# A block of attention and routed experts on one core: the order of the loads before the first expert, and a combination split in two around a VectorE product

## The chip, the cores and the metric

The kernel runs on one core of a Trainium2 chip. The metric is device time in microseconds (us) of one execution. The kernel before took 1906.12 us, the median of 3 runs (1905.55 to 1906.73).

## The reference

Input is x of 4 batches, 1024 rows each, 512 wide (4096 rows, that is 32 tiles of 128 rows). The first half is an attention-like block without softmax over rows (products with 512x512 weights, a shift by one row). What matters here is the second half, a layer of 8 experts with the best 2 chosen for each row, and one shared expert:

```python
h = _layernorm(x) * (1 + cb) + sb
# ffn, with F = 352, FS = 704, E = 8, K = 2
shared_out = (silu(h @ Wsg.T) * (h @ Wsu.T)) @ Wsd.T
scores = softmax(h @ Wr.T)
topk_scores, topk_idx = top_k(scores, 2)
out_e = (silu(h @ Wg[e].T) * (h @ Wu[e].T)) @ Wd[e].T      # for each expert e
routed_out = sum over the two chosen e of topk_scores * out_e
x = x + gb * (routed_out + shared_out)
```

All of it is in float32. The kernel gets it from products of three terms: each operand is split into a high part (rounded by ScalarE) and a low part (the difference, on VectorE), and TensorE adds high*high, high*low and low*high.

## The kernel before

The work of the second half is cut into units. A unit is 128 rows through one set of 352 hidden columns. For each unit TensorE does, in this order: it turns the previous unit's hidden rows (`turn_hid`, 3 transposes, L2027), multiplies this unit's rows with the gate and up weights (`up`, 24 matmuls of 352 columns, L566 to L568), and multiplies the previous unit's turned rows with the down weights (`down`, 9 matmuls, L2032 to L2034). ScalarE does `hidhi` (the high part of the turned rows, L1199) and `silu` (L1205). VectorE does `hidlo` (the low part, L1632) and `hid_of` (the product of silu(gate) and up, called `hid`, L1628). TensorE's next `turn_hid` waits for `hid`, and its `down` waits for `hid_lo`.

The shared expert is two halves of 352 columns, so one tile of rows is two units. Tiles 0 to 13 (FU = 14) are done beside the attention part, tiles 14 to 17 after it (`EARLY`, up to SPLIT = 18), then come the 39 routed tiles of 256 rows (`ROUTED`, two units each, one expert each), and then tiles 18 to 31 of the shared expert (`LATE`). Rows were scattered by expert into a buffer in DRAM (`expert_in_rows`) by GpSimd's indirect DMAs, and results go to `expert_out_rows`.

Before a routed tile can start, its rows must be loaded (`load_rows`, 2 DMAs of 256 KB) and its expert's weights (`load_expert`, 3 DMAs of 1408, 512 and 192 KB, into one of two buffers `raw`), which ScalarE and VectorE then split. All of these are issued by SyncE (SP), in the order of its program. After the last rows are read for the scatter (L837), SP's program before goes: eight pads of zero rows (`pad_rows`, L873 and L874, 512 KB each, one behind each expert's rows), the weights of routed tiles 0 and 1, then fourteen loads of what tiles 0 to 13 have so far (`base`, L897, 256 KB each, each waiting for the one two before it), then a wait for the pads and the scatters, and the rows of routed tile 0. The loop over the routed tiles follows, and behind it fourteen loads of residual rows for tiles 18 to 31 (`load_residual`).

In the LATE part the routed results are combined with the shared ones: 16 pairs of tiles, numbered q. GpSimd gathers the two results of each row (4 indirect DMAs a pair). ScalarE multiplies the first with its score (`first_product`, L1339 and L1342). VectorE adds the second times its score (L1866, two instructions), multiplies by the gate of the batch (L1871) and adds to the base rows (L1881). `combined_at(q)` says at which tile and half this stands, on ScalarE and on VectorE alike; before it is tile 19 + q // 2, half q % 2.

Engines take their instructions in the order written. ScalarE's part of the LATE loop, which the change does not touch, is this:

```python
for half in range(2):
    ...
    hidhi_before(*LATE.before(t, half))
    silu(LATE.unit(t, half), bank_of(LATE, half))
    if half and n + 2 < NT:
        load_turned(LATE, n + 2)
    ...
    for q in range(NT // 2):
        if combined_at(q) == (n, half):
            first_product(q)
```

Of the kernel before, what the change touches and what calls it, by code (L numbers as in the profile page):

```python
# [20 lines left out]
P = 128  # L21
# [4 lines left out]
NT = N // P  # L26
# [8 lines left out]
NJ = (2 * N + E * (R - 1)) // R  # L35
NU = NJ * R // P
FU = 14
SPLIT = 18
# [82 lines left out]
ROUTED = Part(0, NJ, 2 * SPLIT, EARLY)  # L121
# [16 lines left out]

def combined_at(q):

    return SPLIT + 1 + q // 2, q % 2


COMBINED_FIRST = next(q for q in range(NT // 2) if 2 * q + 1 >= combined_at(q)[0])
# [15 lines left out]
def sweep(eng, count, lead, lag, body, first=0):  # L160

    low = first + lag + 2 + lag % 2
    high = count - lead - (count - lead) % 2
    for t in range(first - lead, low):
        body(Tile(None, t, count, first))
    with eng.Fori(0, (high - low) // 2) as k:
        for j in range(2):
            body(Tile(k, low + j, count, first))
    for t in range(high, count + lag):
        body(Tile(None, t, count, first))  # L170
# [6 lines left out]
def one_by_one(part, lead, lag, body):  # L177
    for n in range(part.first - lead, part.count + lag):
        body(Tile(None, n, part.count, part.first))
# [45 lines left out]
def build(nc, io, out):  # L225
# [3 lines left out]
    def scratch(name, shape, dt=F32):  # L229
        return nc.dram_tensor(name, shape, dt).ap()  # L230
# [4 lines left out]
    xres_d = scratch("xres_rows", [N, D])  # L235
# [6 lines left out]
    with ctx:  # L242
        def sem(name):
            return ctx.enter_context(nc.semaphore(name))

        def pair_of_sems(name):
            return [sem(f"{name}{p}") for p in range(2)]
# [46 lines left out]
        first = w1_shelf  # L294
# [121 lines left out]
        base = fourth.put("base", [P, NT, D])  # L416
# [40 lines left out]
        rs_out = sem("rs_out")  # L457
        fb_in = pair_of_sems("fb_in")
# [157 lines left out]
        def load_raw(sp, i, gu_rows, dn_rows):  # L616

            whole = FK - 1
            sp.dma_start(raw[i][:, 0:C * GU], gu_rows).then_inc(raw_in[i], 16)
            sp.dma_start(raw[i][:, C * GU:C * GU + whole * D].rearrange("p (k d) -> p k d", k=whole),  # L620
                         dn_rows[0:whole * P, :].rearrange("(k p) d -> p k d", p=P)).then_inc(raw_in[i], 16)
            sp.dma_start(raw[i][0:F - whole * P, C * GU + whole * D:RAW], dn_rows[whole * P:F, :]).then_inc(raw_in[i], 16)
# [8 lines left out]
        FIRST = ROUTED.tile(0)  # L631
# [8 lines left out]
        def bank_of(part, half):  # L640

            return 0 if part is FUSED else half
# [5 lines left out]
        def _(sp):  # L648
# [181 lines left out]
            def load_scattered(n):  # L830
                if n == 0:
                    sp.wait_ge(route_ones, 2)
                    sp.wait_ge(route_const, 4)
                if n >= 2:
                    sp.wait_ge(sc_out[n % 2], 32 * (n // 2))
                sp.wait_ge(h3_out[n % 2], 16 * (n // 2) + 16)
                sp.dma_start(sc_rows[:, n % 2, :], h3_d[n * P:(n + 1) * P, :]).then_inc(sc_in[n % 2], 16)  # L837
# [21 lines left out]
            def load_residual(n):  # L859
                order = n - FU  # L860
                if order >= 2:
                    sp.wait_ge(sr_in[order % 2], 16 * (order // 2))
                sp.dma_start(base[:, n, :], xres_d[n * P:(n + 1) * P, :]).then_inc(sr_in[order % 2], 16)

            def load_expert(t):
                e = sp.value_load(eid[0:1, bass.ds(t.n, 1)], min_val=0, max_val=E - 1)
                if t.back(2).real():
                    sp.wait_ge(*rw_lo_vec.done(t.back(2).n, "dn_lo"))
                load_raw(sp, t.p, io["ex_gu"][bass.ds(e, 1)].rearrange("a p c -> (a p) c"),
                         io["ex_dn"][bass.ds(e, 1)].rearrange("a f d -> (a f) d"))  # L870
# [14 lines left out]
            for n in range(26, NT):  # L885
                load_scattered(n)
            sp.wait_ge(route_done, 1)
            sp.wait_ge(pads_zero, 1)
            for e in range(E):
                pad_rows(e)  # L890
            for first in range(2):
                load_expert(ROUTED.tile(first))
            sp.wait_ge(rs_out, 16 * FU)
            for n in range(FU):
                if n >= 2:
                    sp.wait_ge(fb_in[n % 2], 16 * (n // 2))
                sp.dma_start(base[:, n, :], xres_d[n * P:(n + 1) * P, :]).then_inc(fb_in[n % 2], 16)  # L897


            def load_rows(t):  # L900
                first = sp.value_load(row_of_tile[0:1, bass.ds(t.n, 1)], min_val=0, max_val=XS_ROWS - R)
# [7 lines left out]
            for p in range(2):  # L909
                sp.wait_ge(sc_out[p], 32 * (NT // 2))  # L910

            def load_shared_again(i):

                t = Tile(None, NJ + i, NJ + 2)
                sp.wait_ge(*rw_lo_vec.done(t.n - 2, "dn_lo"))
                load_raw(sp, t.p, io["sh_gu"][i], io["sh_dn"][i])

            def routed_step(t):
                if t.back(-1).real():
                    load_rows(t.back(-1))  # L920
                if t.real() and t.back(-2).real():
                    load_expert(t.back(-2))
                if t.pair is None and t.n in (NJ - 2, NJ - 1):
                    load_shared_again(t.n - (NJ - 2))

            sweep(sp, NJ, 2, 0, routed_step)


            for n in range(SPLIT, NT):
                load_residual(n)  # L930
            for q in range(COMBINED_FIRST):
                sp.wait_ge(*cb_vec.done(q, "out"))
                sp.dma_start(out_d[2 * q * P:2 * (q + 1) * P, :].rearrange("(a p) d -> p a d", p=P),
# [429 lines left out]
        def _(dve):  # L1363
# [262 lines left out]
            def hid_rows(u, half, bank):  # L1626
                dve.wait_ge(*u_act.done(u, "silu"))
                dve.tensor_tensor(hid[:, half, 0:F], PS_U[bank][:, 0:F], sg_t[:], ALU.mult).then_inc(u_vec.sem_of["hid"], 1)  # L1628
# [154 lines left out]
            def hid_of(part, t, half):  # L1783
                dve.wait_ge(*u_pe.done(part.unit(t, half) - 2, "turned"))
                hid_rows(part.unit(t, half), half, bank_of(part, half))

            def hidlo(part, t, half):
                hidlo_rows(part.unit(t, half))
# [69 lines left out]
            sweep_part(dve, ROUTED, 1, 1, routed_step)  # L1858


            def combine(q):
                p = q % 2
                dve.wait_ge(y2_in[p], 32 * (q // 2) + 32)
                dve.wait_ge(*cb_act.done(q, "first"))
                for a in range(2):
                    last = dve.scalar_tensor_tensor(cb_out[:, p, a, :], cb_y2[:, p, a, :], w2[:, 2 * q + a, :],  # L1866
                                                    cb_out[:, p, a, :], ALU.mult, ALU.add)
                last.then_inc(cb_vec.sem, 1)
                dve.wait_ge(*cb_vec.done(q, "both"))
                batch = q // (TPB // 2)  # L1870
                dve.tensor_tensor(cb_out[:, p], cb_out[:, p], mod3[:, batch:batch + 1, :].to_broadcast([P, 2, D]),  # L1871
                                  ALU.mult).then_inc(cb_vec.sem, 1)
                dve.wait_ge(*cb_vec.done(q, "gated"))
                rows = base[:, 2 * q:2 * q + 2, :]
                if q >= COMBINED_FIRST:
                    for n in range(2 * q, 2 * q + 2):
                        order = n - FU
                        dve.wait_ge(sr_in[order % 2], 16 * (order // 2) + 16)
                else:
                    dve.wait_ge(*base_vec.done(2 * q + 1, "base"))  # L1880
                dve.tensor_tensor(rows if q >= COMBINED_FIRST else cb_out[:, p], cb_out[:, p], rows,  # L1881
                                  ALU.add).then_inc(cb_vec.sem, 1)

            for n in range(SPLIT, NT):
                t = LATE.tile(n)
                for half in range(2):
                    before = LATE.before(t, half)
                    hidlo(*before)
                    hid_of(LATE, t, half)
                    if n == SPLIT:  # L1890
                        expert_lo(Tile(None, NJ + 1, NJ + 2), half)
                    if before[0] is ROUTED:
                        y_of_unit(*before[1:])
                    if n == SPLIT + 1 and not half:
                        for k in range(2):
                            dve.wait_ge(fb_in[k], 16 * len(range(k, FU, 2)))
                    pairs = [q for q in range(NT // 2) if combined_at(q) == (n, half)]
                    for q in pairs:
                        if q >= COMBINED_FIRST:
                            combine(q)  # L1900
                    if before[0] is LATE and not half:
                        base_of(LATE, n - 1)
                    for q in pairs:
                        if q < COMBINED_FIRST:
                            combine(q)
            hidlo(LATE, LATE.last(), 1)
            base_of(LATE, NT - 1)

# [331 lines left out]
```

## Time and profile before

| | |
|---|---|
| median of 3 runs | 1906.12 us |
| the profiled execution | 1902.73 us, its span 1901.0 us |
| mean granted TensorE clock | 0.956 of 2.4 GHz |
| busy share of the span | TensorE (PE) 91%, VectorE (DVE) 71%, ScalarE (ACT) 40%, GpSimd (POOL) 29% |
| chain that ended last | PE 65%, DVE 19%, DMA 5%, issue 4%, POOL 3% |

A PE that is busy 91% of the time leaves little: the places to look at are the stretches where it stands still. The profile names for an idle stretch the instruction behind it and what released that. The clock (PEclk) is what the chip granted: 1.00 is 2.4 GHz and 0.50 is 1.2 GHz.

### The profile page before, as it was taken

Reading aid. Unit: us, or ns where it says so; the run is one execution under the profiler, and the core shown is the slowest. Engines: PE = TensorE matmul, PEld = TensorE weight load, DVE = VectorE, ACT = ScalarE, POOL = GpSimd, SP = SyncE. Lnnn points to the kernel's source line nnn. Section 1 sums busy time; section 2 is a strip of 40 time slices with the busy share of each in tenths; the row PEclk is TensorE's granted clock in tenths of the full one; section 3 lists DMA queues with packets and bytes.
Section 4 is the critical chain, followed back from the end, with each engine's and each line's share of the span. In section 5 each row is a group of like instructions: output and inputs, shape, how many; then the busy total and the mean of one; then the engine's idle time right before and its main releaser. Section 6 shows DMA issues by size and latency. Waiting matters only on the chain.

```text
span 1901.0 us, 28565 instructions
## 1 busy us (share of the span) xinstructions
PE 1726.2 (91%) x9093; PEld 1494.5 (79%) x9093; DVE 1347.9 (71%) x2468; ACT 767.5 (40%) x1147; POOL 548.4 (29%) x631
## 2 busy tenths in 40 slices
PE   4599999997678999999999884999999999997898
PEld 0488888885567878878878784999999999986888
DVE  4899999984587788777776533667666666756752
ACT  2333333341334545545454212455554545432221
POOL 0344444441354434545545420000000000006620
PEclk8699999999789999999999996999999999999999
DMA  9422222211533434545545786766667676677731
GB/s 333 144 91 88 88 88 88 88 66 67 180 111 124 143 139 150 200 151 192 206 147 183 272 287 187 251 237 242 240 233 251 230 255 230 247 243 246 244 118 45
DMA packets 141362, 338.74 MB, mean 178 GB/s; under 512 B 20649, under 2 KB 20649, under 8 KB 135777
## 3 DMA queue, kind: packets, MB, share of 16 engines
q1 hardware_dynamic: 110592, 250.15, 38.4%
q10 hardware_dynamic: 20448, 54.01, 7.7%
q0 software_dynamic: 10240, 33.56, 5.1%
q8 instruction: 42, 0.69, 0.1%
q14 instruction: 40, 0.32, 0.1%
HBM read 230.14 MB, written 107.53 MB: 178 GB/s over the span
## 4 chain that ended last, share of the span: by engine, by line
PE 65%; DVE 19%; DMA 5%; issue 4%; POOL 3%; ACT 2%; SPq 1%; another core or an unknown queue 0%; DVEq 0%; ACTq 0%; POOLq 0%
PE bank L566 16%; PE bank L567 15%; PE bank L568 15%; DVE mix L1544 6%; PE bank L577 4%; PE bank L2032 4%; PE bank L2034 4%; PE bank L2033 4%; PE bank L2027 2%; DVE xm_lo L1550 1%; DMA base<-xres_rows 1%; ACT xm_hi L1147 1%; POOL diff L1000 1%; DMA stage<-in_w_k 1%; DVE k_lo L1557 1%
## 5 line engine op out<-in xcount | busy, mean ns | idle before, releaser
L566 PE MATMUL bank<-gu_hi,ex_x_hl 128*128 128x352 f32 x1136 | 380.3, 335 | 2.7 <-DVE gu_lo L1810 1.9
L568 PE MATMUL bank<-gu_hi,ex_x_hl 128*128 128x352 f32 x1136 | 368.0, 324 | 0.0
L567 PE MATMUL bank<-gu_lo,ex_x_hl 128*128 128x352 f32 x1136 | 367.9, 324 | 0.0
L1081 POOL DMA_INDIRECT raw<-expert_out_rows,out_slots x64 | 74.2, 1159 | 624.7 <-DMA expert_out_rows<-y_rows 588.4
L1628 DVE TENSOR_TENSOR hid<-bank,sg_t 128x352 f32<-128x352 f32 x142 | 74.0, 521 | 231.6 <-ACT sg_t L1205 225.3
L566 PEld LDWEIGHTS bank<-gu_hi,ex_x_hl 128*128 128x128 f32 x1136 | 215.7, 190 | 3.4 <-DVE gu_lo L1810 2.1
L1544 DVE SCALAR_TENSOR_TENSOR mix<-diff,vecs,h2T 128x128 f32<-128x128 f32 x256 | 160.7, 696 | 80.0 <-POOL diff L1000 80.0
L567 PEld LDWEIGHTS bank<-gu_lo,ex_x_hl 128*128 128x128 f32 x1136 | 215.8, 190 | 0.0
L568 PEld LDWEIGHTS bank<-gu_hi,ex_x_hl 128*128 128x128 f32 x1136 | 215.1, 189 | 0.0
L2032 PE MATMUL bank<-dn_hi,hid_hi 128*128 128x512 f32 x426 | 172.7, 405 | 23.5 <-DVE hid_lo L1632 17.2
L1205 ACT ACTIVATE sg_t<-bank 128x352 f32<-128x352 f32 x142 | 66.1, 465 | 306.8 <-PE bank L568 290.7
L2034 PE MATMUL bank<-dn_hi,hid_lo 128*128 128x512 f32 x426 | 170.5, 400 | 0.0
L2033 PE MATMUL bank<-dn_lo,hid_hi 128*128 128x512 f32 x426 | 169.3, 397 | 0.0
L1810 DVE TENSOR_TENSOR gu_lo<-raw,gu_hi 128x2816 fp32r<-128x2816 f32 x41 | 126.4, 3082 | 7.1 <-ACT gu_hi L1281 7.1
L1139 ACT ACTIVATE h2T<-bank,vecs 128x128 f32<-128x128 f32 x128 | 48.2, 457 | 186.0 <-PE bank L577 186.0
L566 PE MATMUL bank<-w_r_hi,xm_hi 128*128 128x512 f32 x256 | 109.0, 426 | 9.9 <-DVE h1T L1467 9.9
L1281 ACT ACTIVATE gu_hi<-raw 128x2816 fp32r<-128x2816 f32 x41 | 105.0, 2560 | 19.8 <-issue 12.5
L2032 PEld LDWEIGHTS bank<-dn_hi,hid_hi 128*128 128x128 f32 x426 | 81.4, 191 | 38.6 <-issue 20.9
L567 PE MATMUL bank<-w_r_lo,xm_hi 128*128 128x512 f32 x256 | 105.8, 413 | 0.0
L568 PE MATMUL bank<-w_r_hi,xm_lo 128*128 128x512 f32 x256 | 105.3, 411 | 0.0
L566 PE MATMUL bank<-w_k_hi,xm_hi 128*128 128x512 f32 x256 | 104.1, 407 | 0.0
L1476 DVE SCALAR_TENSOR_TENSOR stage<-diff,vecs,h1T 128x128 f32<-128x128 f32 x384 | 102.9, 346 | 0.0
(229 smaller groups left out, 3942.0 us busy)
## 6 DMA issues: line engine op xcount, KB each, us to landing
raw<-in_ex_gu SPq DMA_DIRECT2D x39, 1408.0 KB, 6.6
raw<-in_ex_dn SPq DMA_DIRECT2D x39, 512.0 KB, 7.4
ex_x<-expert_in_rows SPq DMA_DIRECT2D x78, 256.0 KB, 2.7
expert_out_rows<-y_rows ACTq DMA_DIRECT2D x78, 256.0 KB, 5.4
h_rows<-h_t SPq DMA_DIRECT2D x64, 256.0 KB, 2.4
h_turned<-h_hl ACTq DMA_DIRECT2D x32, 512.0 KB
ex_x_hl<-h_turned ACTq DMA_DIRECT2D x32, 512.0 KB
x_t<-in_x SPq DMA_DIRECT2D x32, 256.0 KB, 2.6
```

Of the source, the lines that this page charges most:

```text
L566: pe.matmul(acc, act_hi[i], w_hi[i], start=(i == 0), stop=False)
L567: pe.matmul(acc, act_hi[i], w_lo[i], start=False, stop=False)
L568: last = pe.matmul(acc, act_lo[i], w_hi[i], start=False, stop=(i == chunks - 1))
L577: last = pe.transpose(bank[:, c * P:(c + 1) * P], rows[:, c * P:(c + 1) * P], ident[:])
L1081: pool.indirect_dma_start(rows[:, pair % 2, a, :], None, ys_d, bass.IndirectOffsetOnAxis(ap=out_slots[:, k, n:n + 1], axis=0)).then_inc(ar ...
L1281: act.activation(flat_of(gu_hi, t), raw[t.p][:, 0:C * GU], ACT.Copy).then_inc(rw_hi_act.sem, 1)
L1476: last = dve.scalar_tensor_tensor(mix1[:, m, c, :], diff1[:, c, :], vecs[:, mu, c:c + 1], h1T[:, t.p, c, 0:P], ALU.mult, ALU.add)
L1544: last = dve.scalar_tensor_tensor(mix2[:, m, c, :], diff2[:, c, :], vecs[:, mu, c:c + 1], h2T[:, t.p, c, 0:P], ALU.mult, ALU.add)
L1810: dve.tensor_tensor(flat_of(w_lo, t), raw[t.p][:, cols], flat_of(w_hi, t).bitcast(F32), ALU.subtract).then_inc(rw_lo_vec.sem, 1)
L2032: pe.matmul(PS_Y[:], hid_hi[:, c, :], dn_hi[w][:, c, :], start=start and c == 0, stop=False)
L2033: pe.matmul(PS_Y[:], hid_hi[:, c, :], dn_lo[w][:, c, :], start=False, stop=False)
L2034: last = pe.matmul(PS_Y[:], hid_lo[:, c, :], dn_hi[w][:, c, :], start=False, stop=stop and c == FK - 1)
```

## The change

It has three parts.

- SyncE's order ahead of the routed part. The first expert's weights are loaded ahead of the eight pads. Behind the pads come the wait for pads and scatters and the first tile's rows, and only then the second tile's weights. The fourteen loads of `base` and the fourteen residual loads are taken apart: routed step n issues one of them, for n from 0 to 13 and from 18 to 31, behind its weights. SP's loop over the routed tiles is written out (`one_by_one` in the place of `sweep`).
- `combined_at(q)` is one tile later, 20 + q // 2. With it COMBINED_FIRST, from which on the result is added into `base` and stored from there, goes from 12 to 13.
- VectorE's `combine(q)` is cut in two. `weighted(q)` (the two scored additions and the gate) stands between `hidlo` and `hid_of`, and `combined(q)` (the addition to the base rows) behind `hid_of`.

```diff
 def combined_at(q):
-    return SPLIT + 1 + q // 2, q % 2
+    return SPLIT + 2 + q // 2, q % 2
...
             sp.wait_ge(route_done, 1)
+            load_expert(FIRST)
             sp.wait_ge(pads_zero, 1)
             for e in range(E):
                 pad_rows(e)
-            for first in range(2):
-                load_expert(ROUTED.tile(first))
-            sp.wait_ge(rs_out, 16 * FU)
-            for n in range(FU):
-                if n >= 2:
-                    sp.wait_ge(fb_in[n % 2], 16 * (n // 2))
-                sp.dma_start(base[:, n, :], xres_d[n * P:(n + 1) * P, :]).then_inc(fb_in[n % 2], 16)
...
             for p in range(2):
                 sp.wait_ge(sc_out[p], 32 * (NT // 2))
+            load_rows(FIRST)
+            load_expert(ROUTED.tile(1))
+            sp.wait_ge(rs_out, 16 * FU)
+            def load_base(n):
+                if n >= 2:
+                    sp.wait_ge(fb_in[n % 2], 16 * (n // 2))
+                sp.dma_start(base[:, n, :], xres_d[n * P:(n + 1) * P, :]).then_inc(fb_in[n % 2], 16)
...
-                if t.pair is None and t.n in (NJ - 2, NJ - 1):
+                if t.n >= NJ - 2:
                     load_shared_again(t.n - (NJ - 2))
-            sweep(sp, NJ, 2, 0, routed_step)
-            for n in range(SPLIT, NT):
-                load_residual(n)
+                if t.n < FU:
+                    load_base(t.n)
+                elif SPLIT <= t.n < NT:
+                    load_residual(t.n)
+            one_by_one(ROUTED, 0, 0, routed_step)
...
-            def combine(q):
+            def weighted(q):
...
+            def combined(q):
+                p = q % 2
                 dve.wait_ge(*cb_vec.done(q, "gated"))
...
                     hidlo(*before)
+                    for q in pairs:
+                        weighted(q)
                     hid_of(LATE, t, half)
...
                     for q in pairs:
                         if q >= COMBINED_FIRST:
-                            combine(q)
+                            combined(q)
                     if before[0] is LATE and not half:
                         base_of(LATE, n - 1)
                     for q in pairs:
                         if q < COMBINED_FIRST:
-                            combine(q)
+                            combined(q)
```

On SyncE, before, this stood behind the last pad (L897 are the base loads, of which the first three of fourteen are shown):

```order
L874 DMA expert_in_rows<-y_rows 128x2x512
L866 TENSOR_LOAD eid
L866 ISA x2
L619 ISA
L619 DMA raw_177<-in_ex_gu 128x2816
L620 ISA
L620 DMA raw_177<-in_ex_dn 128x2x512
...
L897 DMA base<-xres_rows 128x512 [waits rs_out]
L897 DMA base<-xres_rows 128x512
L897 DMA base<-xres_rows 128x512 [waits fb_in0]
...
L901 TENSOR_LOAD row_of_tile [waits sc_out0,sc_out1,pad_out,h3T_out]
```

And in the changed kernel, with line numbers of its own (L894 and L898 load rows, L912 is the base load of a step):

```order
L874 DMA expert_in_rows<-y_rows 128x2x512
L894 TENSOR_LOAD row_of_tile [waits sc_out0,sc_out1,pad_out,h3T_out]
L894 ISA x2
L898 ISA
L898 DMA ex_x<-expert_in_rows 128x512
L898 ISA
L898 DMA ex_x<-expert_in_rows 128x512
L866 TENSOR_LOAD eid
L866 ISA x2
L619 ISA
L619 DMA raw_178<-in_ex_gu 128x2816
```

The rows of tile 0 moved ahead of the second expert's weights and of all base loads, and only the pads and one expert's weights are still ahead of them.

On VectorE, before, the LATE loop with pairs read like this (L1632 `hid_lo`, L1628 `hid`, L1793 and L1799 the base rows of a tile, L1866 to L1881 the combination of a pair):

```order
L1632 TENSOR_TENSOR hid_lo<-bank,hid_hi 128x384
L1628 TENSOR_TENSOR hid<-bank,sg_t 128x352
L1793 TENSOR_TENSOR gated_t<-bank,mod_179 128x512
L1799 TENSOR_TENSOR base<-base,gated_t 128x512
L1866 SCALAR_TENSOR_TENSOR raw_177<-raw_178,w_149,raw_177 128x512 x2
L1871 TENSOR_TENSOR raw_177<-raw_177,mod_179 128x1024
L1881 TENSOR_TENSOR raw_177<-raw_177,base 128x1024
L1632 TENSOR_TENSOR hid_lo<-bank,hid_hi 128x384
L1628 TENSOR_TENSOR hid<-bank,sg_t 128x352
```

And now (L1635 is `hid_lo`, L1631 `hid`, L1869 and L1874 are `weighted`, L1887 is `combined`):

```order
L1635 TENSOR_TENSOR hid_lo<-bank,hid_hi 128x384
L1869 SCALAR_TENSOR_TENSOR raw_177<-raw_178,w_149,raw_177 128x512 x2
L1874 TENSOR_TENSOR raw_177<-raw_177,mod_179 128x1024
L1631 TENSOR_TENSOR hid<-bank,sg_t 128x352
L1796 TENSOR_TENSOR gated_t<-bank,mod_179 128x512
L1802 TENSOR_TENSOR base<-base,gated_t 128x512
L1887 TENSOR_TENSOR raw_177<-raw_177,base 128x1024
L1635 TENSOR_TENSOR hid_lo<-bank,hid_hi 128x384
L1869 SCALAR_TENSOR_TENSOR raw_177<-raw_178,w_149,raw_177 128x512 x2
```

Three instructions moved from behind `hid` to ahead of it. On ScalarE the order is the one that stood before, here from the changed kernel (L1202 `hidhi`, L1208 `silu`, L1342 and L1345 `first_product`):

```order
L1202 ACTIVATE hid_hi<-bank 128x384 [waits u_pe_turned,u_pe_down]
L1208 ACTIVATE sg_t<-bank 128x352 [waits u_pe_up,u_vec_hid]
L1216 DMA ex_x_hl<-h_turned 128x1024
L1342 ACTIVATE act_col<-eps 128x1 [waits y1_in1,final_out1]
L1345 ACTIVATE raw_177<-raw_178,w_148 128x512 x2
```

The first product of a pair stands behind the `silu` of the same unit, as before; the whole block came one tile later.

## Rows read from the trace of the kernel before

**Rows 1.** Timeline of PE (start us, us, instruction, [idle before it, releaser]), routed start.
```profile
1164.81 1.11 PE L577 MATMUL bank<-ident,ex_x 128*128 128x128 f32 x4 [25.69 <-DMA ex_x<-expert_in_rows]
...
1184.16 0.49 PE L2027 MATMUL bank<-ident,hid 128*128 128x128 f32 x3
```

**Rows 2.** Chain that ended last (start us, us, what), SyncE's work before the routed part.
```profile
1115.63 0.80 SPq L873
...
1129.01 0.61 SPq L866
...
1161.91 2.86 DMA ex_x<-expert_in_rows
```

**Rows 3.** Timeline of SyncE's queue, the base loads and one expert load in the loop.
```profile
1134.20 26.79 SPq L897 DMA_DIRECT2D base<-xres_rows  x14
...
1199.11 0.33 SPq L619 DMA_DIRECT2D raw<-in_ex_gu  x1
```

**Rows 4.** Windows: length, busy us (instructions) by engine, PEclk, DMA share, GB/s.
```profile
1120.00:1130.00 10.00, 10.00 (x62) 9.49 (x61) 2.93 (x5) 1.45 (x3) 0.99 (x2) 1.00 1.00 370
1200.00:1300.00 100.00, 100.00 (x602) 93.63 (x601) 68.30 (x74) 49.78 (x60) 0.00 (x0) 1.00 0.71 247
```

**Rows 5.** Timeline of ACT, the split of gate and up weights, tiles 0 and 3.
```profile
1139.35 2.55 ACT L1281 ACTIVATE gu_hi<-raw 128x2816 fp32r<-128x2816 f32 x1 [5.56 <-DMA raw<-in_ex_dn]
...
1209.18 2.56 ACT L1281 ACTIVATE gu_hi<-raw 128x2816 fp32r<-128x2816 f32 x1
```

**Rows 6.** The page's DMA issues: KB each, median us to landing.
```profile
raw<-in_ex_dn SPq DMA_DIRECT2D x39, 192.0 KB, 8.3
```

**Rows 7.** Timeline of PE in the LATE part.
```profile
1704.94 0.49 PE L2027 MATMUL bank<-ident,hid 128*128 128x128 f32 x3
...
1721.66 0.77 PE L2032 MATMUL bank<-dn_hi,hid_hi 128*128 128x512 f32 x1 [6.12 <-issue]
...
1741.74 0.49 PE L2027 MATMUL bank<-ident,hid 128*128 128x128 f32 x3
...
1748.00 0.49 PE L2027 MATMUL bank<-ident,hid 128*128 128x128 f32 x3
...
1754.14 0.47 PE L2032 MATMUL bank<-dn_hi,hid_hi 128*128 128x512 f32 x1 [1.81 <-DVE hid_lo L1632]
...
1892.84 0.49 PE L2027 MATMUL bank<-ident,hid 128*128 128x128 f32 x3
```

**Rows 8.** Timeline of DVE in the LATE part.
```profile
1717.12 1.41 DVE L1866 SCALAR_TENSOR_TENSOR raw<-raw,w,raw 128x512 f32<-128x512 f32 x2 [4.06 <-DMA raw<-expert_out_rows,out_slots]
...
1746.74 0.53 DVE L1628 TENSOR_TENSOR hid<-bank,sg_t 128x352 f32<-128x352 f32 x1 [2.02 <-issue]
...
1749.60 1.41 DVE L1866 SCALAR_TENSOR_TENSOR raw<-raw,w,raw 128x512 f32<-128x512 f32 x2
...
1752.31 1.23 DVE L1881 TENSOR_TENSOR raw<-raw,base 128x1024 f32<-128x1024 f32 x1
1753.45 0.55 DVE L1632 TENSOR_TENSOR hid_lo<-bank,hid_hi 128x384 fp32r<-128x384 f32 x1
...
1754.63 1.41 DVE L1866 SCALAR_TENSOR_TENSOR raw<-raw,w,raw 128x512 f32<-128x512 f32 x2 [0.20 <-ACT raw L1342]
```

**Rows 9.** Timeline of ACT in the LATE part, tile 21 half 0, tile 21 half 1.
```profile
1746.17 0.47 ACT L1205 ACTIVATE sg_t<-bank 128x352 f32<-128x352 f32 x1 [3.35 <-PE bank L568]
...
1746.63 1.33 ACT L1342 ACTIVATE raw<-raw,w 128x512 f32<-128x512 f32 x2
...
1753.19 1.34 ACT L1342 ACTIVATE raw<-raw,w 128x512 f32<-128x512 f32 x2
```

**Rows 10.** PE behind an idle stretch, in its timeline.
```profile
1109.24 0.76 PE L2032 MATMUL bank<-dn_hi,hid_hi 128*128 128x512 f32 x1 [3.92 <-DVE hid_lo L1632]
```

**Rows 11.** Windows, columns as in rows 4: behind that stretch, and in the attention part.
```profile
500.00:560.00 60.00, 38.35 (x165) 30.42 (x166) 47.04 (x84) 25.26 (x39) 30.24 (x38) 0.85 0.24 88
1109.20:1114.70 5.50, 5.46 (x15) 4.51 (x16) 3.11 (x9) 0.49 (x1) 2.31 (x3) 0.50 0.58 213
```

More of the change, by code:

```diff
@@ L920, in routed_step @@
                     load_rows(t.back(-1))
-                if t.real() and t.back(-2).real():
+                if t.back(-2).real():
                     load_expert(t.back(-2))
-                if t.pair is None and t.n in (NJ - 2, NJ - 1):
+                if t.n >= NJ - 2:
                     load_shared_again(t.n - (NJ - 2))
-            sweep(sp, NJ, 2, 0, routed_step)
-            for n in range(SPLIT, NT):
-                load_residual(n)
+                if t.n < FU:
[3 more added lines that the diff above has]
+            one_by_one(ROUTED, 0, 0, routed_step)
             for q in range(COMBINED_FIRST):
@@ L1887, in _ @@
                     before = LATE.before(t, half)
+                    pairs = [q for q in range(NT // 2) if combined_at(q) == (n, half)]
+                    if n == SPLIT + 2 and not half:
+                        for k in range(2):
+                            dve.wait_ge(fb_in[k], 16 * len(range(k, FU, 2)))
                     hidlo(*before)
+                    for q in pairs:
+                        weighted(q)
                     hid_of(LATE, t, half)
@@ L1893, in _ @@
                         y_of_unit(*before[1:])
[L1894 to L1897, printed above, removed]
                     for q in pairs:
                         if q >= COMBINED_FIRST:
-                            combine(q)
+                            combined(q)
                     if before[0] is LATE and not half:
```

## The prediction

> **What bounds the kernel now.** I read the busy shares and the slices first: PE is busy 91% of the span, so a gain can only come from stretches in which it stands still. PE's timeline, read for its bracketed idle times, then shows two places that this change touches. The first is the start of the routed part. PE sits idle 25.69 us until the first rows have landed, and turns them at 1164.81 [rows 1]. The chain of waits runs back from there through SyncE: pads from 1115.63 to 1129.01, two loads of expert weights to 1134.20, base loads to 1160.99, rows issued at 1161.91 and landed 2.86 us later [rows 2, 3]. The weights were not what was late: ScalarE had begun on them at 1139.35 [rows 5]. Between the two places PE is busy 100 of 100 us at the full clock [rows 4], so nothing is won there.
>
> The second place is the LATE part. The turn of a unit's hidden rows marks its start T. A unit that waits for nothing takes 1748.00 - 1741.74 = 6.26 us [rows 7]. From the turn at 1704.94 to the last one at 1892.84 lie 26 units in 187.90 us, where 26 * 6.26 = 162.8. So 25.1 us are lost there in waits, most of them behind the combination of pairs: `hid_lo` comes at 1753.45, behind three combination instructions, and PE starts `down` only at 1754.14, after 1.81 us idle; once it is 6.12 us, where VectorE waited 4.06 us for gathered rows [rows 7, 8].
>
> **The start.** SyncE is free at 1115.63. One set of weights takes (1134.20 - 1129.01) / 2 = 2.6 us to issue and the eight pads 13.4 us [rows 2, 3], so the last pad is issued at about 1131.6. The routed rows then wait for the pads to land. Weights (2112 KB) and pads (8 * 512 KB) are 6.4 MB, 17 us at the 370 GB/s that the queues moved with full DMA engines [rows 4], besides the last scatters. Before, the same pads and the same weights, in the other order, had all landed when ScalarE started at 1139.35 [rows 5]. That is the late bound; the early one is the last issue plus some 2 us, 1133.6. I take 1138.3, close to the late bound since the bytes are the same. From there to the issue of the rows is about 0.9 us (1161.91 - 1160.99), and 2.9 us to landing: 1142.1 in place of 1164.8, a gain of 22.7 us. PE ends its EARLY work at 1164.81 - 25.69 = 1139.12, so the gain cannot be over 25.7.
>
> What is late next is the second expert's weights. They go out behind the rows, last issue near 1145, and land up to 8.3 us after issue [rows 6], at worst 1151 to 1153. ScalarE's program has their split (2.55 us, rows 5) ahead of `hidhi`, and PE's first `down` waits for that. In this first unit PE has some 8 us of turns and `up` to do. I price this at 0 and leave 0 to 4 us for it. Behind it the two first units take what they took (1184.16 - 1164.81 = 19.35 us, partly at the low clock [rows 1]), perhaps a little less.
>
> **Loads spread over the routed steps.** A step issues one more DMA of 256 KB, 0.7 us of transfer at 370 GB/s, behind the weights, in a stretch where the DMA share is 0.71 [rows 4]. Weights issued at 1199.11 land about 8.3 us after their last issue (1.1 us later), near 1208.5, and are wanted at 1209.18 [rows 3, 5, 6]. That cover is under 1 us, but the extra load is queued behind the weights on the same queue. I take 0, and 0 to 1 us a step if it gets in their way. The residual loads no longer stand behind the loop; nobody waits for them early, so 0.
>
> **The combination, one tile later.** Gathers end where they ended before, so the first pair finds its rows there, 12.5 us later than before. The 6.12 us idle and its follow-ups go. I count the whole 25.1 us of loss as gone and put the new losses in.
>
> **The combination, cut in two.** `weighted(q)` now stands on VectorE ahead of `hid` of the same unit, and it waits for ScalarE's first product of pair q. ScalarE has this behind `silu` of the same unit. So `hid`, which needed only `silu`, now also waits for the first product and for the three `weighted` instructions, and PE's next turn waits for `hid`. Per unit with a pair:
> - from T to `silu`: 1746.17 - 1741.74 = 4.43 us [rows 7, 9];
> - from there to the end of the first product: 1746.63 + 1.33 - 1746.17 = 1.79 [rows 9];
> - to `weighted`: 1754.63 - (1753.19 + 1.34) = 0.10 [rows 8, 9];
> - `weighted`: 1752.31 - 1749.60 = 2.71 [rows 8];
> - `hid`: 0.53 [rows 8];
> - its release to PE, by the nearest such step, `hid_lo` end 1754.00 to `down` 1754.14: 0.14 [rows 7, 8].
>
> The sum is 9.70 us, 3.44 over 6.26. There are 16 such units: 55.0 us. `combined` (1.2 us) and the base rows of a tile fall into the idle time after `hid` and end before the next `hid_lo` is wanted: they cost nothing in a unit this long.
>
> VectorE might be asked whether it could take `hid` ahead of the waiting `weighted`. The trace says no: `hid_lo` stayed behind the 4.06 us wait and PE stood 6.12 us [rows 7, 8]. The Trainium skill, "TensorE: Matmul & The Clock Gate", section "Architectural detail: the array is 16× 32×32, not 1× 128×128", says that ScalarE's and VectorE's queues are strictly first in, first out. By that rule the 55.0 us stand, and without it they would be 0; the trace agrees with the rule.
>
> **The clock.** 3.44 us of idle in each unit is new. After 3.92 us idle at 1105.3 the next 5.5 us ran at a granted 0.50, that is 1.2 GHz [rows 10, 11], while after 1.81 us it mostly stayed at 2.4 GHz. With busy work 5.5 us at the half rate cost 2.75 us. A stretch much like the new one is 500 to 560: PE busy 38.35 of 60 us, 64% (here 6.26 / 9.70 = 65%), and a mean clock of 0.85 [rows 11], so 30% of the time at the low level; of a unit of some 11.4 us that is 3.4 us, and half of it, 1.7 us, is lost if PE works in it. `up` lies on the chain above, so most of that counts. Bounds: 0 and 2.75 us. I take 1.7, 27 us over 16 units.
>
> **The sum.** -22.7 - 25.1 + 55.0 + 27.2 = +34.4 us. On the profiled execution (span 1901.0, itself 1902.73 against the median of 1906.12) the span becomes 1935.4. On the median it is 1940.5.
>
> **Rivals.**
> - *The clock holds.* The same chain without the 27.2: +7.2, 1913. For it: 1.81 us of idle left the clock alone in most units. Against: rows 10 and 11.
> - *The clock is low through all of* `up` *each time.* 2.75 us a unit or slightly more: +51, 1957 and up to 1962 with a weak start.
> - *Faster.* The place is VectorE's wait in `weighted`. If it finds ScalarE's product done, its 2.7 us fit into the 3 us that VectorE idles before `hid`, and only some 0.5 us a tile remains: -22.7 - 25.1 + 4 = -44, 1862. It would need the first product ahead of `silu`; the code order says otherwise. A weaker form decides by price: the start and the old losses give 47.8, so below 47.8 / 16 = 3.0 us a unit the kernel is faster. At 3.44 without a clock penalty it is just above.
> - *The spread loads push the weights.* 28 steps at up to 1 us on top of the forecast: 1955 to 1968. Against: they are queued behind.
> - *The change at the start does nothing,* since the pads are waited for until the old time. They are issued by 1131.6 and 25 us of base loads are gone from ahead of the rows, so I give this next to nothing.
>
> **Numbers.** Forecast 0.70; clock holds 0.10; clock low throughout 0.11; faster 0.04; spread loads 0.05. The forecast's own range is 1928 to 1952 (start 18 to 25, clock 1.2 to 2.2 us a unit). To leave out no more than 2 in 10 I take 1918 to 1958. About 0.2% is what a measurement of this kernel can tell from no change: faster by more 0.05, within 0.03, slower 0.92.
>
> **What would show it.** Right: PE's first turn of routed rows near 1142; turns spaced 9.7 us or more in the 16 units with a pair, `hid` directly behind `weighted`, PE's idle time ahead of L2027 released by `hid`, about 3.4 us each; PEclk under 0.9 in those slices; gathers never late. Wrong: turns 6.3 us apart there (`weighted` not waiting), a clock of 1.00 through the LATE part (then 1913), or idle time of ScalarE for weights in the routed loop.

## The result, and the profile after

| | median us | runs | ratio to before, 95% interval |
|---|---|---|---|
| before | 1906.42 | 4 (1905.55 to 1907.44) | |
| changed | 1938.26 | 4 (1936.40 to 1946.47) | 1.0183 (1.0165 to 1.0201) |

The change made the kernel 31.8 us slower by the medians. The ratio is not that of the medians; it stands for 34.9 us of 1906.4. The profiled execution is the longest of its four, 1946.47 us with a span of 1944.7, while the profiled one of before, 1902.73, is under all four of its own. Differences between the two traces (43.7 us of span) are therefore larger than those between the medians, and the text says which of them it uses.

PE's timeline of the changed kernel at the routed start, the answer to [rows 1] (start us, us, instruction, idle before it and its releaser):

```profile
1144.58 1.11 PE L577 MATMUL bank<-ident,ex_x 128*128 128x128 f32 x4 [5.62 <-DMA ex_x<-expert_in_rows]
...
1157.58 0.50 PE L2040 MATMUL bank<-dn_hi,hid_hi 128*128 128x512 f32 x1 [3.25 <-DVE hid_lo L1635]
...
1168.49 0.49 PE L2035 MATMUL bank<-ident,hid 128*128 128x128 f32 x3
```

The first rows are there 20.2 us earlier. Part of that is lost in the next 24 us: the turn that stood at 1184.16 now stands at 1168.49, 15.7 us earlier. SyncE's queue and ScalarE's timeline tell why (the answers to [rows 2, 3] and [rows 5]):

```profile
1120.30 11.08 SPq L874 DMA_DIRECT2D expert_in_rows<-y_rows  x8
1141.88 0.94 SPq L898 DMA_DIRECT2D ex_x<-expert_in_rows  x2
1143.58 0.34 SPq L619 DMA_DIRECT2D raw<-in_ex_gu  x1
```

```profile
1133.53 2.55 ACT L1284 ACTIVATE gu_hi<-raw 128x2816 fp32r<-128x2816 f32 x1
...
1153.30 2.55 ACT L1284 ACTIVATE gu_hi<-raw 128x2816 fp32r<-128x2816 f32 x1 [5.54 <-DMA raw<-in_ex_dn]
...
1156.24 0.48 ACT L1202 ACTIVATE hid_hi<-bank 128x384 fp32r<-128x384 f32 x1
```

The first weights no longer wait (1133.53 in place of 1139.35). The last pad is issued at 1131.4 and the rows only at 1141.88, when the pads have landed. The second expert's weights go out behind the rows and land at 1153.30. ScalarE waits 5.54 us for them, with the high part of the hidden rows behind it in its program, and that is PE's 3.25 us.

In the routed part nothing is lost. Of PE's waits between 1180 and 1660 not one is listed. The spread base and residual loads cost nothing that can be seen.

The LATE part is where the time went. PE's timeline, the answer to [rows 7], is first the turn of tile 19, then the turns of units with a pair:

```profile
1688.88 0.49 PE L2035 MATMUL bank<-ident,hid 128*128 128x128 f32 x3
...
1701.40 0.49 PE L2035 MATMUL bank<-ident,hid 128*128 128x128 f32 x3
...
1710.96 0.52 PE L2035 MATMUL bank<-ident,hid 128*128 128x128 f32 x3 [3.16 <-DVE hid L1631]
...
1722.20 0.79 PE L2035 MATMUL bank<-ident,hid 128*128 128x128 f32 x3 [3.27 <-DVE hid L1631]
...
1756.95 0.88 PE L2035 MATMUL bank<-ident,hid 128*128 128x128 f32 x3 [3.17 <-DVE hid L1631]
...
1884.04 0.87 PE L2035 MATMUL bank<-ident,hid 128*128 128x128 f32 x3 [3.26 <-DVE hid L1631]
```

Tile 19 starts 16.1 us earlier than before and its two units take 6.26 us each: the gather wait is gone. Then come 16 units in 1884.04 - 1701.40 = 182.6 us, 11.4 us each. The first of them, still at the full clock, takes 9.56. A group of three transposes takes 0.49 us at 2.4 GHz and 0.88 at 1.2. ScalarE and VectorE around the turn at 1756.95, the answers to [rows 9] and [rows 8]:

```profile
1751.82 0.47 ACT L1208 ACTIVATE sg_t<-bank 128x352 f32<-128x352 f32 x1 [4.89 <-PE bank L568]
1752.18 0.20 ACT L1342 ACTIVATE act_col<-eps 128x1 f32<-128x1 f32 x1
1752.27 1.32 ACT L1345 ACTIVATE raw<-raw,w 128x512 f32<-128x512 f32 x2
```

```profile
1753.70 1.42 DVE L1869 SCALAR_TENSOR_TENSOR raw<-raw,w,raw 128x512 f32<-128x512 f32 x2 [6.18 <-ACT raw L1345]
1755.15 1.22 DVE L1874 TENSOR_TENSOR raw<-raw,mod 128x1024 f32<-128x1024 f32 x1
1756.29 0.52 DVE L1631 TENSOR_TENSOR hid<-bank,sg_t 128x352 f32<-128x352 f32 x1
```

VectorE stands still for 6.18 us, waiting for a product that ScalarE can only do behind `silu`. `hid` could have run from 1752.3 on; it starts at 1756.29, behind `weighted`. PE's waits from 1690 to 1895 are one line, and the window of the 16 units, the answer to [rows 11], shows the clock (length, busy us by PE, weight loads, DVE, ACT, POOL, PEclk, DMA share, GB/s):

```profile
PE bank L2035 <- DVE hid L1631: 51.3, 16, 3.3
```

```profile
1701.40:1884.00 182.60, 131.30 (x577) 120.13 (x575) 85.08 (x112) 37.09 (x80) 75.80 (x58) 0.81 0.48 149
```

Sixteen waits, 51.3 us, and a mean granted clock of 0.81. Of PE's 131.3 busy us only 16 * 6.26 = 100.2 would be needed at 2.4 GHz.

### The profile page after: what moved, and what is told of

Its sections match the earlier page's. It is cut to its first block, busy times and chain, and to the rows that moved or that the text cites. A ratio compares the mean times of both kernels' runs of the same rounds, so it can differ in the third digit from the quotient of the medians.

```text
span 1944.7 us, 28391 instructions
## 1 busy us (share of the span) xinstructions
PE 1754.3 (90%) x9093; PEld 1522.8 (78%) x9093; DVE 1345.7 (69%) x2468; ACT 767.5 (39%) x1147; POOL 556.6 (29%) x631
## 4 chain that ended last, share of the span: by engine, by line
PE 66%; DVE 19%; issue 5%; ACT 4%; DMA 3%; POOL 2%; SPq 1%; DVEq 0%; ACTq 0%; POOLq 0%
PE bank L566 17%; PE bank L567 16%; PE bank L568 16%; DVE mix L1547 5%; PE bank L577 4%; PE bank L2042 3%; PE bank L2040 3%; PE bank L2041 3%; PE bank L2035 2%; DVE xm_lo L1553 1%; ACT xm_hi L1150 1%; DVE raw L1869 1%; DVE hid L1631 1%; POOL diff L1003 1%; ACT raw L1345 1%
## 5 line engine op out<-in xcount | busy, mean ns | idle before, releaser
L566 PE MATMUL bank<-gu_hi,ex_x_hl 128*128 128x352 f32 x1136 | 395.0, 348 | 4.3 <-DMA ex_x_hl<-h_turned 2.4
L567 PE MATMUL bank<-gu_lo,ex_x_hl 128*128 128x352 f32 x1136 | 381.1, 335 | 0.0
L568 PE MATMUL bank<-gu_hi,ex_x_hl 128*128 128x352 f32 x1136 | 380.2, 335 | 0.0
L1084 POOL DMA_INDIRECT raw<-expert_out_rows,out_slots x64 | 83.0, 1296 | 659.4 <-DMA expert_out_rows<-y_rows 569.8
L566 PEld LDWEIGHTS bank<-gu_hi,ex_x_hl 128*128 128x128 f32 x1136 | 227.7, 200 | 4.8 <-DMA ex_x_hl<-h_turned 2.7
L567 PEld LDWEIGHTS bank<-gu_lo,ex_x_hl 128*128 128x128 f32 x1136 | 227.2, 200 | 0.0
L568 PEld LDWEIGHTS bank<-gu_hi,ex_x_hl 128*128 128x128 f32 x1136 | 226.0, 199 | 0.0
L1631 DVE TENSOR_TENSOR hid<-bank,sg_t 128x352 f32<-128x352 f32 x142 | 73.9, 521 | 214.0 <-ACT sg_t L1208 211.2
L1208 ACT ACTIVATE sg_t<-bank 128x352 f32<-128x352 f32 x142 | 66.1, 466 | 332.0 <-PE bank L568 331.7
L2035 PE MATMUL bank<-ident,hid 128*128 128x128 f32 x426 | 75.6, 289 | 51.9 <-DVE hid L1631 51.9
L1202 ACT ACTIVATE hid_hi<-bank 128x384 fp32r<-128x384 f32 x142 | 68.8, 484 | 120.6 <-PE bank L2035 118.6
L2035 PEld LDWEIGHTS bank<-ident,hid 128*128 128x128 f32 x426 | 54.3, 148 | 65.1 <-issue 58.9
```

Of the source, the lines that this page charges most:

```text
L566: pe.matmul(acc, act_hi[i], w_hi[i], start=(i == 0), stop=False)
L567: pe.matmul(acc, act_hi[i], w_lo[i], start=False, stop=False)
L568: last = pe.matmul(acc, act_lo[i], w_hi[i], start=False, stop=(i == chunks - 1))
L1084: pool.indirect_dma_start(rows[:, pair % 2, a, :], None, ys_d, bass.IndirectOffsetOnAxis(ap=out_slots[:, k, n:n + 1], axis=0)).then_inc(ar ...
L2035: last = pe.transpose(PS_H[:, c * P:(c + 1) * P], hid[:, half, c * P:(c + 1) * P], ident[:])
```

## The experiments

Each ratio is to the kernel before, run on the same chip beside it. The changed kernel was not run again beside them, so a comparison with it goes through the ratios, the medians or the traces, and these differ by several us.

| kernel | median us | ratio, 95% interval |
|---|---|---|
| 1: SyncE's order alone | 1884.56 | 0.9882 (0.9865 to 0.9898) |
| 2: combination alone | 1956.84 | 1.0259 (1.0241 to 1.0276) |
| 3: changed, first product a unit earlier | 1861.16 | 0.9772 (0.9751 to 0.9792) |
| 4: changed, PE's idle time filled | 1916.20 | 1.0045 (1.0029 to 1.0061) |
| 5: changed, combination in one piece | 1878.30 | 0.9855 (0.9839 to 0.9871) |
| 6: changed, first product ahead of silu | 1863.67 | 0.9786 (0.9768 to 0.9804) |
| 7: 3, hidden rows' high part ahead of weights | 1860.45 | 0.9763 (0.9748 to 0.9777) |
| 8: 3, both experts' weights ahead of the pads | 1866.96 | 0.9789 (0.9773 to 0.9805) |
| 9: 7, the first two products in their own unit | 1861.09 | 0.9763 (0.9750 to 0.9777) |
| 10: 6 and 7 together | 1860.81 | 0.9758 (0.9745 to 0.9772) |

**1 and 2, each half of the change by itself.** Kernel 1 is the kernel before with the changed kernel's SyncE program. Kernel 2 is the kernel before with the changed `combined_at` and VectorE's two parts:

```diff
 # kernel 2, against the kernel before; SyncE's program untouched
-    return SPLIT + 1 + q // 2, q % 2
+    return SPLIT + 2 + q // 2, q % 2
...
-            def combine(q):
+            def weighted(q):
...
+            def combined(q):
```

> The kernel before with SyncE's new order alone (weights, pads, rows, then the spread loads); combination as before. Theory: the routed part starts some 16 us earlier, as in the changed kernel where PE's turn at the head of tile 19 came at 1688.88 in place of 1704.94, and the late part is unchanged: 1906.4 - 16 = 1890 us. Rival (the spread loads slow the routed steps, and are the cost of the change): PE idles in the routed steps and the time is 1906 or above.

> The kernel before with the later and split combination alone, SyncE as before. Theory: the 26 late units take 247.7 us in place of 187.9, so 1906.4 + 59.8 = 1966 us, within 8 us by where the low clock falls. Rival (the slowdown comes from SyncE's part): near 1906 us or below.

Kernel 1 is 22.3 us faster between the medians (16.5 between the profiled spans, 1884.5 and 1901.0). Its late part is that of before, 188.4 us from the turn of tile 19 to the last one, against 187.9. Kernel 2 is 50.0 us slower (59.5 between the spans), with 16 waits for `hid` in its profile:

```profile
PE bank L2032 <- DVE hid L1628: 51.3, 16, 3.3
PE bank L577 <- DMA ex_x<-expert_in_rows: 32.1, 1, 32.1
```

Between the medians the halves are worth -22.3 and +50.0, together +27.7, where the whole measured +31.8. Between the spans it is -16.5 and +59.5, together +43.0 against +43.7. By the ratios it is +26.9 against +34.9, and these 8 us are a little more than the three intervals of 3.1 to 3.4 us to each side explain together. The traces add up closely, the times only roughly. Both expectations, set from the traces, were too high: kernel 1 by 5 us, and kernel 2 by 9, which is outside its 8. But the signs and the sizes leave no room for the rival of either run: SyncE's part is a gain and the combination is the loss.

**3 and 6, the product earlier.** Kernel 3 changes only when ScalarE does the first product:

```diff
-                        if combined_at(q) == (n, half):
+                        if 2 * combined_at(q)[0] + combined_at(q)[1] == 2 * n + half + 1:
                             first_product(q)
```

Kernel 6 leaves it in its unit and moves the same loop from behind `silu` to between `hidhi` and `silu`.

> The changed kernel with ScalarE's first product of a pair one unit earlier, so that it is done before VectorE comes to the scored additions. Theory (VectorE waits for ScalarE's product behind silu): the 16 units fall from 11.4 to 6.3 to 6.7 us, 16 * 4.9 = 78 us and the 2.6 us of the unit behind them less: about 1858 us, 1852 to 1868. Rival (the 2.7 us of additions ahead of hid are too much for VectorE by themselves): units stay over 9 us and the time above 1900.

> The changed kernel with ScalarE's first product in the same unit, but ahead of silu in place of behind it. Theory: the product ends some 2.5 us behind the unit's start, the scored additions at 5.3, hid at 5.9, in time for the next turn at 6.3: as the kernel with the product a unit earlier, 1861 us, 1858 to 1868. Rival (only a product of an earlier unit is early enough, as silu and hid are late now): units over 7 us, 1875 us or more.

Both do what the theory asks. In kernel 3 the 26 late units take 164.2 us in place of 247.7, nearly the 162.8 that they need at the least. VectorE of kernel 3:

```profile
1725.96 0.56 DVE L1635 TENSOR_TENSOR hid_lo<-bank,hid_hi 128x384 fp32r<-128x384 f32 x1 [1.53 <-ACT hid_hi L1202]
1726.43 1.41 DVE L1869 SCALAR_TENSOR_TENSOR raw<-raw,w,raw 128x512 f32<-128x512 f32 x2
1727.87 1.23 DVE L1874 TENSOR_TENSOR raw<-raw,mod 128x1024 f32<-128x1024 f32 x1
1729.01 0.52 DVE L1631 TENSOR_TENSOR hid<-bank,sg_t 128x352 f32<-128x352 f32 x1
```

The same three instructions stand in the same order as in the changed kernel, but `weighted` follows `hid_lo` at once and fills the time in which VectorE would wait for `silu`. The rival, that VectorE's own work ahead of `hid` is too much, falls: what cost 77 us between the medians was the wait in front of it. That `silu` only has to be passed, and not a whole unit, kernel 6 shows (165.5 us).

**4, the idle time filled.** The waits stay, but PE works through most of each. This kernel does matmuls whose results nothing reads:

```diff
                     down(*before)
+                    if any(combined_at(q) == (n, half) for q in range(NT // 2)):
+                        for _ in range(FILL):      # 12
+                            pe.matmul(PS_X[:], hid_hi[:, 0, :], dn_hi[0][:, 0, :], start=True, stop=True)
```

> The changed kernel with 12 matmuls of 128x512 more behind the down product of each of the 16 units with a pair, into a bank that nothing reads, so that PE works in its idle time. The wait for hid stays. Theory (idle time of 3.2 us lets the clock fall, which costs 1.7 us a unit): units of 9.6 to 9.8 us at 2.4 GHz, 16 * 1.7 + 2.6 = 30 us less than the changed kernel: 1908 us, 1903 to 1914. Rival (the units are 11.4 us long for another reason, a longer chain or late transfers): 1938 us or more.

Two turns of kernel 4, and a window over its units with a pair:

```profile
1731.42 0.52 PE L2036 MATMUL bank<-ident,hid 128*128 128x128 f32 x3 [0.41 <-DVE hid L1632]
...
1741.11 0.52 PE L2036 MATMUL bank<-ident,hid 128*128 128x128 f32 x3 [0.51 <-DVE hid L1632]
```

```profile
1703.00:1858.00 155.00, 147.59 (x775) 128.53 (x774) 86.24 (x113) 37.59 (x81) 75.64 (x57) 1.00 0.56 175
```

The clock is 1.00 throughout and the units are 9.57 to 9.70 us long. The late part is 216.7 us against 247.7, 31.0 less, with more work in it. Between the ratios it is 1.0183 - 1.0045, or 26 us, and between the medians 22. The expected 1908 was missed by 8 us, and 1916.20 is outside its 1903 to 1914. It had been set 30 us below the changed kernel's median with terms from its profiled execution, whose low clock seems to have been costlier than usual: in kernel 2's trace, with the same 16 waits, the clock stayed high behind two of them (units of 9.59 and 9.60 us), and the late part is 242.0. That is an argument from two traces; the medians' own traces do not exist.

**5, the later place without the cut.** SyncE's new order and one tile later, but the whole combination behind `hid` as before.

> The changed kernel with the combination in one piece again behind hid, but one tile later. Theory: the gather wait of the first pair is gone (13.4 to 6.3 us for that unit), the whole combination still lies ahead of the next hid_lo in each tile's first half and costs 2 to 3 us a tile: 1884.6 (SyncE's order alone) - 7 = 1877 us, 1872 to 1881. Rival (the later place alone gives all that there is): 1862 us or less.

As forecast. The gather wait is gone, and each tile's first half still pays for a combination ahead of `hid_lo`. Against kernel 1 this is 0.9855 to 0.9882, some 5 us for the later place. From kernel 5 to kernel 3 it is 0.9855 to 0.9772, some 16 us for the cut, once the product comes early. PE's waits in the late part of kernel 5 and of kernel 3:

```profile
PE bank L2035 <- DVE hid_lo L1635: 15.8, 9, 2.0
```

```profile
PE bank L2040 <- DVE hid_lo L1635: 1.2, 1, 1.2
PE bank L2035 <- DVE hid L1631: 0.3, 1, 0.3
```

**7 and 8, the start.** Kernel 7 takes `hidhi` of the first routed unit out from behind the weights that are late:

```diff
+                    first_unit = t.only(0) and not half
+                    if not first_unit:
                         expert_hi(t.back(-1), half)
...
                     hidhi_before(*ROUTED.before(t, half))
+                    if first_unit:
+                        expert_hi(t.back(-1), half)
```

Kernel 8 has instead `load_expert(ROUTED.tile(1))` directly behind `load_expert(FIRST)`, ahead of the pads.

> As the kernel with the product a unit earlier, and in the first routed unit ScalarE does the rows' and hidden rows' high parts ahead of the split of the second expert's weights. Theory (PE's 3.25 us idle ahead of the first down is hid_hi queued behind weights that land at 1153.3): that idle time goes, and 0 to 1.5 us of low clock with it: 3 to 5 us less than 1861, so 1857 us. Rival (the weights are then late for the next thing in line, silu): 1861 us, no gain.

> As the kernel with the product a unit earlier, with both experts' weights ahead of the pads and the rows behind them; the base loads stay spread. Theory (pads and rows go by the bytes ahead of them): the rows land 5 to 6 us later, near 1150, but no weights are late behind them, which gives 3 to 5 us back: 1862 us, 1860 to 1866. Rival (the order of weights is all, and base loads ahead of the rows cost nothing): near the old start, 1875 us or more.

In kernel 7's trace the 3.25 us ahead of the first `down` are gone (0.4 and 1.1 us of waits stand in the unit behind), and two units later PE is 20.1 us behind its first turn of rows, where kernel 3 is 21.6 and the changed kernel 23.9. Its median does not tell it from kernel 3 (the intervals overlap). The rival was half right, as the weights are then waited for a little with `silu` behind them. In kernel 8 the rows are turned at 1149.27, 5.7 us later than in kernel 3, as the bytes ahead of them say, and no weights are waited for. Two units later PE is 18.6 us behind that turn, so in the traces the start as a whole loses 2.7 us. The median is 5.8 us above kernel 3's and outside the 1860 to 1866 that was expected, though the ratios, 0.9789 and 0.9772, lie within each other's intervals. The rest of the difference between the two traces, 4.9 us, lies in the late part (169.1 us), behind 6.73 us in which ScalarE stands still ahead of `silu` at 1709.21 and for which the profile names no engine or queue of this core. So the record does not show how much of the 5.8 us the start costs. The order of the second weights is worth little either way. What made the start faster is that the base loads no longer stand ahead of the rows: with both experts' weights ahead of them, as before, kernel 8's rows are still turned 15.5 us earlier than the 1164.81 of the kernel before.

**9 and 10, towards a best version.** Kernel 7's trace had some 3.4 us lost at tiles 19 and 20 (units of 7.13 and 8.81 us). The expectation of kernel 9 puts them down to ScalarE, a unit ahead, waiting for the first gathered rows. The trace does not bear this out: ScalarE does both products of pair 0 from 1695.79 to 1697.11 without a wait, `silu` was already late at 1695.23 with no product ahead of it, and for the 3.82 us ahead of `hidhi` at 1700.93 the profile names no engine or queue of this core. Their cause stays open. Kernel 9 leaves pairs 0 and 1 in their own unit, ahead of `silu`; kernel 10 does so with all.

> The kernel with hid's high part ahead of the second expert's weights, and with the products of pairs 0 and 1 in their own unit ahead of silu, all others a unit earlier. Theory (a product a unit ahead puts ScalarE into the wait for the first gathered rows, which cost 3.5 us at tiles 19 and 20 of that kernel's profile): that goes, and the rest stays: 1857 us, against 1860.5 of the kernel with all products a unit earlier. Rival (the 3.5 us were that one execution's): 1860 us, no change.

> The same start, all products in their own unit ahead of silu. Theory: no gather wait either, but 1 to 2 us more over the 16 units than with a product a unit ahead (165.5 against 164.2 us for the 26 late units): 1858 to 1859 us. Rival (hid's high part first gives nothing): as with the products ahead of silu alone, 1863 us.

Kernels 7, 9 and 10 cannot be told apart, and kernel 9's expected 1857 did not come. Its late part is 165.4 us against kernel 7's 167.5, but its first rows were turned 3.9 us later. That fits its rival, that the 3.5 us belonged to one execution. Across the nine profiles with the same SyncE program PE turned the first rows anywhere from 1140.4 to 1146.0 (1149.3 in kernel 8). This spread of 5.6 us is larger than what kernels 7, 9 and 10 differ in. It is there before the first weights are issued: this happens at 1113.3 to 1119.9, and from there to the turn it is 25.4 to 27.1 us in all nine. Kernels 7, 9 and 10 each beat both kernels, by 44 to 46 us against the kernel before.

## Why the prediction was right

The forecast was 1940.5 us within 1918 to 1958, and the median is 1938.26. It is right in its mechanism too: the order of the waits, their number and the low clock behind them came as forecast. That the median lies within 2.3 us of it is in part luck. The forecast was worked out on traces, and there it gave +34.4 where +43.7 was measured. Both parts missed to the same side: the start gave 16.1 us and not 22.7, and the late part cost 59.8 and not 57.1. Between the medians the start gave 22.3, nearly as forecast, and the late part, in kernel 2, only 50.0.

- *The start, -22.7.* Kernel 1 measured -22.3. The steps behind it were less exact. The rows came 2.5 us later than I took (1144.58 against 1142.1). The last pad was issued on time, at 1131.4, but the rows only at 1141.88 and not at 1139.2. SyncE had come to this place 1.2 us later (its last load for the scatter ends at 1116.69 against 1115.52), and the rest, some 1.5 us, is the landing of the pads. The second expert's weights landed at 1153.30, in the "at worst" that I had priced at 0 with 4 us left for it; in the trace this was 20.2 us of head start against 15.7 two units later, a loss of some 4.5. The medians came out at the forecast all the same. That fits a start that varies by several us: with SyncE's old program the first rows were turned at 1164.81 in one trace and at 1168.90 in kernel 2's, and the forecast stood on the earlier one. But no trace of a median execution shows it.
- *The spread loads, 0.* No PE wait in the whole routed part.
- *The old losses, -25.1.* They went in kernel 3, where the late part takes 164.2 us against 187.9, that is 23.7 less. That the later place removes the gather wait is kernel 5.
- *The wait for ScalarE's product, +55.0.* The sum of 9.70 us a unit is nearly met where the clock is high: 9.57 to 9.70 in kernel 4, 9.64 in the mean, and 9.56 in the changed kernel's first such unit. PE's wait was 3.2 us and not 3.44. Moving the product (kernels 3 and 6) removes it, and VectorE's queue did not pass over the waiting `weighted`.
- *The clock, +27.2.* The mean over the 16 units of the profiled execution is 11.4 us, 1.7 above 9.70; with the clock at 1.00 (kernel 4) the gain was 22 us by the medians, 26 by the ratios and 31.0 in the traces. The sum left out the unit behind the 16, which takes 8.83 us in the place of 6.26. The estimate came from a stretch of the attention part with a like share of idle time, and held. The rival in which the clock holds fell with the granted 0.81.
- *Late terms together.* I had +57.1. In the trace it is 247.7 - 187.9 = 59.8, in kernel 2's trace 54.1, and in the medians of kernel 2 +50.0. The term that is too large for the median execution is probably the clock's, since the low clock came behind 16 of 16 waits in one trace and behind 14 of 16 in the other; this stays open.

The faster rival named its own condition, a first product ahead of `silu`, and 1862 us. That kernel exists as number 6, at 1863.67.

## What to carry to other kernels

Before work is moved ahead of a critical instruction on an in-order engine, list what it waits for and look up where that stands on the other engine: work that fits into an idle gap by its length can still carry a wait that ends behind the gap. It is free only if its inputs are there when the gap begins, and the fix is often to move the producer, not the work. Price a recurring wait on PE twice, once as idle time and once for the low clock in the work behind it. And measure the halves of a change apart: a loss of 50 us hid a gain of 22 here, and one call made earlier turned +1.8% into -2.3% (kernel 3) or -2.1% (kernel 6).

## What the runs showed of the hardware that was not expected

- With 3.2 us of idle time in every unit of some 9.6 us, the granted clock fell to 0.5 behind all 16 waits in the changed kernel's trace (a transpose group of 0.49 us takes up to 0.88) and behind 14 of the same 16 in kernel 2's. Twelve matmuls without use in each gap brought it back to 1.00 and made the kernel 22 us faster by the medians, with more work on PE.
- Weights, pads and first rows, issued one behind the other, took 25.4 to 27.1 us from the first issue to PE's first turn in nine traces of one SyncE program. The time of the first issue varied by 6.6 us, with the loads for the scatter ahead of it. Kernels that differ by 1 to 3 us at such a place were not told apart in five rounds.
- In two traces ScalarE stood still in the late part for 3.82 and 6.73 us (kernels 7 and 8), and in the trace of the kernel before for 5.80 us ahead of `silu` at 1732.65, with a releaser that the profile does not know. No run here shows what it is.
- The pads are the next bound: issued by 1131.4 and landed some 10 us later (SyncE waits 9.7 us for them), with PE waiting 5.62 us for the rows behind them, and 2.7 to 9.1 us over the nine traces. No kernel here moved or shortened them.
